# A dynamic convolution on one core: 85 scratch products in place of 52 between the first mix and the first conv group

## The reference

```
pooled = jnp.mean(x, axis=(2, 3))
att = sigmoid(pooled @ att_w.T + att_b)
agg_w = jnp.einsum('nk,kocij->nocij', att, weight)
out = vmap(conv_one)(x, agg_w)        # 3x3, padding 1, one image with its own weights
...
x = x + conv(_gn(x))
```

## Time and profile before

| | |
|---|---|
| median of 3 runs | 1297.59 us |
| lowest and highest | 1294.86, 1297.61 us |
| the profiled execution's own time | 1296.35 us |
| its span | 1294.6 us |
| mean granted TensorE clock | 0.997 |

### The profile page before, as it was taken

The page is one execution under the profiler, slowest core; times in us unless marked ns, Lnnn a source line. Parts: engine busy times, 40 slices in busy tenths (PEclk is TensorE's granted clock), DMA queues, the critical chain, the costliest instruction groups (busy, mean ns, idle before and its releaser), DMA issues.

```text
span 1294.6 us, 22528 instructions
## 1 busy us (share of the span) xinstructions
PE 1257.6 (97%) x8592; PEld 720.9 (56%) x8592; DVE 1184.9 (92%) x1793; ACT 944.0 (73%) x1537; POOL 74.2 (6%) x99
## 2 busy tenths in 40 slices
PE   1799999999999999999999999999999999999999
PEld 0355555555555555555555555555555555555555
DVE  7999999999999998989999898998989899898993
ACT  5976796977868777786867778686877868778531
POOL 0000000000000000000000000000000000000000
PEclk9899999999999999999999999999999999999999
DMA  9315735457544545535255553545535355553345
GB/s 378 128 66 154 211 83 144 156 150 219 134 119 114 152 129 154 154 75 145 89 153 153 132 140 87 127 129 153 153 75 153 92 145 150 153 136 77 86 110 146
DMA packets 31210, 178.13 MB, mean 138 GB/s; under 512 B 3712, under 2 KB 4224, under 8 KB 28800
## 3 DMA queue, kind: packets, MB, share of 16 engines
q1 hardware_dynamic: 20880, 117.49, 24.6%
q0 software_dynamic: 8928, 49.78, 22.7%
q10 hardware_dynamic: 1296, 9.44, 1.7%
HBM read 115.87 MB, written 51.38 MB: 129 GB/s over the span
## 4 chain that ended last, share of the span: by engine, by line
PE 96%; ACT 2%; DMA 1%; issue 0%; DVE 0%; SPq 0%; ACTq 0%; DVEq 0%
PE pM L491 88%; PE pG L463 8%; DMA W<-w_dram 1%; ACT Us L1144 1%; ACT G L1089 0%; ACT Vs L1037 0%; ACT X L1095 0%; SPq L388 0%; ACT unused L1109 0%; ACT Us L1052 0%; ACT L1136 0%; ACT L1128 0%; ACT unused L1117 0%; ACT small L1136 0%; DVE Us L665 0%
## 5 line engine op out<-in xcount | busy, mean ns | idle before, releaser
L491 PE MATMUL pM<-Vs,Us 128*128 128x385 f16 (+1 forms) x6912 | 1146.0, 329 | 6.6 <-DVE Us L665 6.4
L491 PEld LDWEIGHTS pM<-Vs,Us 128*128 128x128 f16 x6912 | 673.9, 98 | 481.1 <-issue 19.1
L1037 ACT CAST Vs<-E 128x784 f16<-128x784 f32 x192 | 159.2, 842 | 141.2 <-PE pM L491 61.5
L615 DVE SCALAR_TENSOR_TENSOR T<-X 128x784 f32<-128x784 f32 x192 | 180.2, 966 | 16.3 <-ACT X L1095 15.0
L670 DVE TENSOR_TENSOR Vs<-E,Vs 128x784 f16<-128x784 f32 x192 | 182.1, 968 | 3.9 <-ACT Vs L1037 3.8
L1052 ACT ACTIVATE Us<-E 128x768 f16<-128x768 f32 x120 | 98.3, 847 | 85.8 <-DVE E L652 85.4
L463 PE MATMUL pG<-W,D 128*32 128x512 f16 (+1 forms) x1628 | 107.3, 412 | 27.3 <-DVE D L750 26.5
L638 DVE SCALAR_TENSOR_TENSOR E<-T 128x784 f32<-128x784 f32 x128 | 119.1, 972 | 2.2
L652 DVE SCALAR_TENSOR_TENSOR E<-G,T 128x768 f32<-128x768 f32 x128 | 116.9, 955 | 2.2
L1117 ACT ACTIVATE unused<-X,small 128x784 int8<-128x784 f32 x120 | 113.9, 949 | 3.9
L665 DVE SCALAR_TENSOR_TENSOR Us<-E,Us 128x768 f16<-128x768 f32 x120 | 111.9, 952 | 1.6
(11 more groups left out here) (81 smaller groups left out, 587.9 us busy)
## 6 DMA issues: line engine op xcount, KB each, us to landing
X<-x_cols_dram SPq DMA_DIRECT2D x64, 840.0 KB, 5.8
X<-x_flat_dram POOLq DMA_DIRECT2D x62, 784.0 KB, 7.6
out_dram<-X SPq DMA_DIRECT2D x62, 784.0 KB, 4.1
W<-w_dram SPq DMA_DIRECT2D x9, 1024.0 KB, 19.3
G<-W ACTq DMA_DIRECT2D x9, 1024.0 KB, 7.2
X<-x_flat_dram SPq DMA_DIRECT2D x2, 784.0 KB, 5.0
out_dram<-X SPq DMA_DIRECT2D x2, 392.0 KB, 2.3
out_dram<-X SPq DMA_DIRECT2D x4, 196.0 KB, 1.9
```

Source lines behind the costliest of these rows:

```text
L491: mm = pe.matmul(bank(k, o)[:, TR * first:TR * last], Us[:, j, a, c, o, kx, :], v_in(j, b, c, kx), start=(at < 2 and i == 0), stop=(i == 3 ...
L615: return dve.scalar_tensor_tensor(out=dst, in0=a, scalar=scale, in1=d, op0=ALU.mult, op1=ALU.add)
L1037: act.copy(v_out(j, 0), e_buf(n, ("V", chunk, j))).then_inc(v_hi, 1)
```

## The change

`keep_clock` issues 85 products in place of 52 (and as many weight loads). Nothing else differs; the instructions of the other engines and their order are the same.

```diff
@@ -546,7 +546,7 @@
             mix_tile(0, 6)
             mix_tile(0, 7)
             mix_tile(0, 8)
-            keep_clock(52)
+            keep_clock(85)
             group(0, 0, 0)
             group(0, 0, 1)
             group(0, 1, 0)
```

## The result

The changed kernel took 1299.85 us (median of 14 runs, 1296.95 to 1302.3) against 1297.13 for the kernel before (14 runs, 1294.86 to 1297.81): ratio 1.0023, 95% interval 1.0015 to 1.003. The prediction was 1297.3 with a range from 1294.8 to 1298.1; it is wrong. The profiled execution took 1300.56 us.

What follows compares the result with a forecast made beforehand. TensorE was taken to bound the kernel, VectorE close behind. Cold clock gone -2.65, new wait +2.3, gain lost behind VectorE +0.07: -0.3 us, so 1297.3 us from the median of 1297.59; range 1294.8 to 1298.1.

Steps and rivals of the forecast that it cites:

- What bounds the kernel, and the wait that follows: TensorE bounds the end, VectorE close behind; third group of epoch 0 waits 2.3 us for the sixth low half.
- I take it to stay at 1.00 through the first conv groups.: Clock after the added products: a 1.05 us rest is too short for a fall; worth at most 2.8 us.
- Their own cost on the path is nothing: The 33 added products take 5.4 us before the first group, hidden by TensorE's wait for VectorE: zero cost.
- no instruction of another engine moves.: First group's gate: its low half of the weights still ends at 52.50 us, other engines' instructions unmoved.
- VectorE's own pace in epochs 1 to 4: From 131.77 us VectorE keeps 78.2 us per epoch without waiting for TensorE; only its 0.28 us gain is kept.
- The sign that the forecast named for this case: Third group at 60.9 but end moved over a microsecond would mean VectorE's pace after 131 us was misjudged.
- The wait of 0.28 us before the take: VectorE's wait for TensorE before 131.77 us: would vanish, moving VectorE up by 0.28 us.
- the L665 instruction of 139.31: VectorE's low half for group (1,0) of epoch 1: would come at about 139.0 us.
- Rival B: At the early groups' cold stretch: the whole 2.8 us reaches the end, 1294.8 us; chance 0.08.
- Rival C: Rest before the first group: clock falls in spite of its shortness, products run cold, 1297.6 us; chance 0.09.
- Rival D: Before the first group: added products overrun at half clock, third group 1.5 us later, 1299.1 us; chance 0.05.
- The sum: At the third group -2.65 for the clock and +2.3 new wait; with +0.07 after VectorE's following, -0.3 us at the end.

Runs made afterwards that it cites:

- f2: Kernel before with 97 products of 337 columns in place of its 52, as long as 85 of 384: 1298.96 us, ratio 1.0008.
- g2: Changed kernel with 190 waiting instructions in front, so that all that follows stands 256 places later than before: 1298.87 us, ratio 1.0014.
- e3: Kernel before with 85 products of 235 columns in place of 52 of 384: 1300.19 us, ratio 1.0027.
- g1: Kernel before with 66 instructions at the start of TensorE's program that wait for a semaphore already reached: 1300.16 us, ratio 1.0032.
- h2: Kernel before with 66 waiting instructions spread over the groups of epoch 0 from the third on: 1299.83 us, ratio 1.0019.
- f3: Kernel before with 84 products of 384 and 512 columns in place of 52, some in the new wait: 1298.23 us, ratio 1.0011.
- f1: Changed kernel measured again, nothing altered, against the kernel before: 1299.19 us, ratio 1.0021.
- e2: Changed kernel with 12 more products between groups (0,1) and (1,0) of epoch 0: 1297.3 us, ratio 1.0000 to the kernel before.
- g4: e2 with 166 waiting instructions in front: 1296.72 us, ratio 0.9999 to the kernel before.

## Why the prediction was wrong, point by point

- **What bounds the kernel, and the wait that follows.** Right. The third group was gated by the sixth low half, 8.25 us after the first (8.25 by the forecast's 60.9 and 52.65), with 2.17 us of wait.
- **"I take it to stay at 1.00 through the first conv groups."** This step failed first. The argument looked at the rest of 1.05 us alone. The 2.3 us wait that the same prediction put 6 us later was not asked what it does to the clock. It brings the fall back, at a worse place: the old cold stretch lay before the gate of the sixth low half, which hid 2.3 of its 2.65 us; the new one lies behind that gate, and nothing hides it. With 12 products in the wait the clock stays up and the fourth group is 0.4 us earlier than before, as forecast. The price is 1.3 us at the fourth group and 1.0 to 1.8 us in the time (f2 and g2).
- **"Their own cost on the path is nothing", "no instruction of another engine moves."** This failed second: the term was put at nothing. 33 products are 66 instructions, and all of TensorE's program behind them stands 66 places later. With the clock of before, e3, g1 and h2 put that at 2.5 to 4.1 us; f3, with 64 and the clock at 1.00 in ten of twelve executions, at 1.4, not clear of zero. How much of it the changed kernel pays beside the clock's part no run measures alone; the difference below gives 1.7 us, and f1's twelve executions hardly tell it from f2's. By what path the place costs is open.
- **VectorE's own pace in epochs 1 to 4.** The forecast read there that the products' gain can only be kept as far as VectorE follows. The other half was missed: VectorE's pace hangs on the next image's sums, and those on its loads. In the changed kernel's profile ScalarE waits 0.54 us for the image, VectorE 1.05 us longer for the sums, and TensorE then 0.5 and 0.6 us. The sign that the forecast named for this case (third group at 60.9, the end over a microsecond later) would lay all of the loss on this pace after 131 us; 1.31 us of it was there by the fourth group and lay on TensorE. The wait of 0.28 us before the take, which was to go, is still there (at 134.44), and the L665 instruction of 139.31 comes 1.31 us later, not 0.3 earlier, counted from the first group.
- **Rival B**, the whole 2.8 us. It fell with the gate. **Rival C**, no effect of the short rest, fell too: the clock outlived that rest in the profiles of the changed kernel, e2, f1, f2, f3, g2 and g4. **Rival D** had the right sign by a wrong mechanism; the added products did not overrun.
- **The sum.** Forecast -0.35 at the third group; measured -0.36 there (8.25 against 8.61), then +1.66 for the cold stretch behind it, which makes the 1.3 of the fourth group. 0.23% are 3.0 us, so 1.7 are left for the place of the instructions. That is a difference; the experiments that measure it alone give more on the whole.
- **The chances.** 0.04 for slower was too small because every term was priced at the place of the change.

## What to carry to other kernels

When a rest is filled so that the clock stays up, ask of each wait that the faster engine now runs into what the clock does there, and whether a gate still stands behind the cold stretch; a cold stretch ahead of a gate may cost almost nothing, the same one behind it costs its full price. Instructions added to a long straight program are never only themselves: they move all that stands behind them. Here 66 that do nothing cost 2.5 to 4.1 us, and 50, 90 or 128 nothing measurable, by a path that stays open. Before the cause of a few microseconds is told, run the same instruction count without the effect (thin products, satisfied waits), and the same effect with another count.

## What the runs showed of the hardware that was not expected

- In the changed kernel the granted clock fell 1.2 us after a wait of 2.17 us had ended, behind 36 products at full clock and a rest of 1.06 us before them. With the wait filled by 12 products (e2_fill12) the mean clock was 1.000 in all eleven executions. In the changed kernel it stayed low for 3.41 us; after the old rest of 6.4 us it stayed low for 6.8 (51.34 to 58.16 in the trace). In two of the 14 executions of the changed kernel the mean clock was 1.000 (1298.97 and 1296.95 us), in eleven 0.999 (mean 1300.41), in one 0.998.
- 66 instructions that do nothing, in 26 us of idleness, made the kernel slower by 4.1 us (ratio 1.0032; by medians 3.1); 90 of them by 0.6 (1.0005, not clear of zero).
